# The value image of a deformable convolution, laid out by columns instead of rows

## The reference

```python
# layer 0: on xn = group_norm(x)
offsets = conv3x3(xn, offset_w); mod = 1 + tanh(conv3x3(xn, mod_w))
v = conv1x1(xn, kv_w)[:, C:]                    # the value image, 256 channels
sampled = bilinear(v, px = x + offset_x, py = y + offset_y) * mod   # 4 groups of 64 channels
x = x + conv1x1(sampled, out_w)
# layer 1: on xn = group_norm(x)
x = x + whiten(xn)     # mean and covariance in groups of 16 channels over the whole batch
```

## Time and profile before

| | |
|---|---|
| runs | 6293.51, 6298.68, 6304.76 us |
| median | 6298.68 us |
| span of the profiled execution | 7345.4 us, 66304 instructions |
| time recorded beside that span for the profiled execution | none but the span itself |
| mean granted TensorE clock | 0.796 |
| DRAM traffic | 1612.78 MB |

### The profile page before, as it was taken

The page is one execution under the profiler, slowest core; times in us unless marked ns, Lnnn a source line. Parts: engine busy times, 40 slices in busy tenths (PEclk is TensorE's granted clock), DMA queues, the critical chain, the costliest instruction groups (busy, mean ns, idle before and its releaser), DMA issues.

```text
span 7345.4 us, 66304 instructions
## 1 busy us (share of the span) xinstructions
PE 4556.6 (62%) x16380; PEld 2756.0 (38%) x16380; DVE 4512.5 (61%) x10805; ACT 979.6 (13%) x2075; POOL 4008.4 (55%) x4115
## 2 busy tenths in 40 slices
PE   5665666666666666665666666665667634337876
PEld 3333433343433343333334434343444422224322
DVE  7665666666766666666666656665666644446654
ACT  1111111111111111111111111111111101100000
POOL 0266666666666666565666666665666666660000
PEclk9877777887877878777888777777887766667999
DMA  8865666666666666666666656665666544445999
GB/s 279 277 195 195 222 216 194 221 220 212 220 205 212 216 203 223 206 210 203 199 216 222 211 195 217 211 205 183 195 198 200 186 139 134 127 130 229 421 421 415
DMA packets 931602, 1612.78 MB, mean 220 GB/s; under 512 B 80944, under 2 KB 605872, under 8 KB 929456
## 3 DMA queue, kind: packets, MB, share of 16 engines
q0 software_dynamic: 196608, 537.13, 22.5%
q10 hardware_dynamic: 595968, 536.90, 21.7%
q1 hardware_dynamic: 138928, 537.74, 21.5%
HBM read 1074.58 MB, written 536.87 MB: 219 GB/s over the span
## 4 chain that ended last, share of the span: by engine, by line
DVE 38%; another core or an unknown queue 27%; issue 16%; PE 7%; ACTq 6%; DMA 3%; DVEq 2%; ACT 1%; POOL 0%; SPq 0%; POOLq 0%
DVE patch L614 13%; DVE patch L619 7%; ACTq L1278 6%; DVE vring L497 3%; DVE bst L430 3%; DVE xr_mem L634 3%; DVE taps L509 2%; PE psO L1032 2%; PE psA L1000 2%; DVE samp_mem L625 1%; DVE weight L591 1%; DMA xs_mem<-x_dram 1%; DVE p_w L585 1%; ACT sampT L1179 1%
## 5 line engine op out<-in xcount | busy, mean ns | idle before, releaser
L899 POOL DMA_INDIRECT patch<-v,index_now x4096 | 4002.5, 977 | 2590.3 <-issue 1602.3
L1000 PE MATMUL psA<-wB,xa_mem 128*128 128x364 f32 x3824 | 1503.2, 536 | 768.4 <-issue 443.9
L614 DVE TENSOR_TENSOR patch<-patch,psI 128x512 f32<-128x512 f32 x2048 | 1264.9, 678 | 110.7 <-issue 55.2
L1000 PEld LDWEIGHTS psA<-wB,xa_mem 128*128 128x128 f32 x3824 | 780.7, 216 | 1363.7 <-issue 694.8
L1032 PE MATMUL psO<-sampT,wO_sb 128*128 128x512 f32 x2048 | 1171.5, 710 | 190.5 <-issue 181.4
L497 DVE TENSOR_TENSOR vring<-psA,biasB 128x256 f32<-128x256 f32 x956 | 397.7, 416 | 1375.2 <-remote 1198.7
L1046 PE MATMUL psT<-ident,xr_mem 128*128 128x128 f32 x2048 | 375.2, 334 | 886.3 <-DVE xr_mem L634 394.7
L1032 PEld LDWEIGHTS psO<-sampT,wO_sb 128*128 128x128 f32 x2048 | 456.1, 234 | 718.8 <-issue 709.2
L619 DVE TENSOR_TENSOR patch<-patch 128x512 f32<-128x512 f32 x1024 | 665.3, 691 | 94.7 <-remote 45.9
L1060 PE MATMUL psG<-x1T 128*128 128x129 f32 x4096 | 613.1, 306 | 154.2 <-issue 118.6
L634 DVE SCALAR_TENSOR_TENSOR xr_mem<-psO,bo_sb,xr_mem 128x512 f32<-128x512 f32 x512 | 361.1, 744 | 507.9 <-remote 411.2
(11 more groups left out here) (214 smaller groups left out, 2680.4 us busy)
## 6 DMA issues: line engine op xcount, KB each, us to landing
v<-vring ACTq DMA_DIRECT2D x128, 2048.0 KB
xa_mem<-x_dram SPq DMA_DIRECT2D x128, 1024.0 KB
xr_mem<-x_dram SPq DMA_DIRECT2D x128, 1024.0 KB
x<-xr_mem ACTq DMA_DIRECT2D x128, 1024.0 KB
xs_mem<-x_dram SPq DMA_DIRECT2D x112, 1024.0 KB
patch<-v,index_now POOLq DMA_INDIRECT x4096
patch<-x SPq DMA_DIRECT2D x64, 1024.0 KB, 13.1
out_dram<-patch ACTq DMA_DIRECT2D x64, 1024.0 KB, 32.6
```

The costliest lines, as they stand in the source:

```text
L614: times = eng.tensor_tensor(part, part, w4, ALU.mult)
L899: eng.indirect_dma_start(out=patch[n][:, t, :], out_offset=None, in_=v2_flat[k], in_offset=bass.IndirectOffsetOnAxis(ap=index_now[n][:, t: ...
L1000: mm = eng.matmul(conv_bank[wide][r][:, 0:NA], xa[m][j][:, c, r * W:(r + 1) * W], wB[:, c, :], start=(c == 0), stop=(c == CC - 1))
```

## The change

An entry of `v2` now holds a column and its right neighbour at one row, and the entries stand by columns: column, group, row. Two entries one after the other are rows y0 and y0+1 with both columns, again 1 KB for each sample. The gathers are the same in number and size; their address arithmetic has other factors, and the four weights stand in another order (corners 2 and 3 swapped). A column takes 256 KB (65536 numbers) and is followed by a gap of 2 KB (512 numbers), so neighbouring partitions write and read 264192 bytes apart, where it was 512 bytes.

The neighbour half of an entry is another partition's data. So ScalarE's copy within a partition is replaced by a product with the shift matrix on TensorE (`next_column`, 4 for each pair, 512 columns each) into a bank `psT`, and ScalarE copies it from there (`column_out`). `psT` was used by the two turns before; the new `_free` waits on TensorE order the three uses. The store of a pair is one run of 4 KB for each column and group, 512 runs of the same 2 MB. VectorE no longer waits for ScalarE's copy at the last row of a ring. Some set-up goes, two small DMAs fill the gaps once, and 16 semaphores of the output pass become one.

```diff
-VROW = G * W * ENT
-IMG = VROWS * VROW
+VCOL = G * H * ENT
+VPITCH = VCOL + 2 * PATCH
+IMG = W * VPITCH
...
-        vring = [sb(f"vring{m}", [P, QR + 1, G, 2, CG]) for m in range(2)]
+        vring = [sb(f"vring{m}", [P, G, QR, 2, CG]) for m in range(2)]
...
-                    if row == QR - 1:
-
-                        eng.wait_ge(v_dup, (b * PAIRS + i) * 5 + 2)
-                    dst = vring[m][:, row + 1, :, 0, :]
+                    dst = vring[m][:, :, row, 0, :]
...
-                    a[:, :, G:2 * G], float(VROW), ia, ALU.mult, ALU.add))
+                    a[:, :, G:2 * G], float(ENT), ia, ALU.mult, ALU.add))
...
+            def next_column(b, i, m, q, j, h):
+
+                eng.wait_ge(v_rows[j][h], b * PAIRS + i + 1)
+                eng.matmul(v_now[h], shift[:, 2, :], v_half(m, j, h, 0), start=True, stop=True)\
+                   .then_inc(shifted[j][h], 1)
...
-            def dup(b, i, m, j, rows):
-
-                low = j * ROWS + rows[0]
-                eng.wait_ge(v_row, (b * PAIRS + i) * QR + low + len(rows))
-                if low == 0:
-                    eng.activation(vring[m][:, 0, :, 0, :], vring[1 - m][:, QR, :, 0, :], ACT.Copy)\
-                       .then_inc(v_dup, 1)
-                eng.activation(vring[m][:, low:low + len(rows), :, 1, :],
-                               vring[m][:, low + 1:low + len(rows) + 1, :, 0, :], ACT.Copy)\
-                   .then_inc(v_dup, 1)
+            def column_out(b, i, m, j, h):
+
+                eng.wait_ge(shifted[j][h], b * PAIRS + i + 1)
+                eng.activation(v_half(m, j, h, 1), v_now[h], ACT.Copy).then_inc(v_next[j][h], 1)
...
-                eng.wait_ge(v_dup, (b * PAIRS + i) * 5 + 6)
-                eng.dma_start(v2_rows[k][:, bass.ds(row, 2 * NJ), :],
-                              vring[m][:, 0:QR, :, :, :].rearrange("p r g k e -> p (r g) (k e)"))\
+                eng.wait_ge(v_next[1][1], b * PAIRS + i + 1)
+                eng.dma_start(v2_cols[k][:, :, bass.ds(row, QR), :],
+                              vring[m][:, :, :, :, :].rearrange("p g r k e -> p g r (k e)"))\
```

More of the change, by code:

```diff
@@ L189, in deform_zca_kernel @@
         y_ld = [sem(f"y_ld{j}") for j in range(NY)]
[L190 removed]
+        y_mm = sem("y_mm")
         y_add = [sem(f"y_add{j}") for j in range(NY)]
@@ L272, in deform_zca_kernel, with v_half, before @@
         weight_now = psI[:, 512 - 2 * NJ * 4:512]
+        v_now = [bank[:, :].rearrange("p (g r e) -> p g r e", g=G, e=CG) for bank in psT]
+        def v_half(m, j, h, k):
+            low = j * ROWS + 2 * h
+            return vring[m][:, :, low:low + 2, k, :]
+        def before(b, i, m, q, j):
+            return (b, i, m, q, 0) if j == 1 else (b, i - 1, 1 - m, q - 1 + m, 1)
         block = ctx.enter_context(nc.Block())
@@ L328, in _ @@
                 eng.dma_start(dst, src).then_inc(const_ld, 16)
+            for gap in v2_gaps:
+                eng.dma_start(gap, x_v[0, :, 0, 0:VPITCH - VCOL]).then_inc(const_ld, 16)
             for n, store in enumerate((*v_st, *x1_st)):
@@ L1093, in pair @@
                             if three is not None:
+                                if turned:
+                                    next_column_free(*last_conv, 1)
+                                    if prepare and j == 1:
+                                        next_column_free(*last_conv, 0)
                                 turn_x1(*three)
@@ L1098, in pair @@
                                 conv((2,))
+                            if alongside and ca is not None:
+                                if three is not None:
+                                    x1_free(*three, 0)
+                                else:
+                                    next_column_free(*last_conv, 0)
+                                next_column(*here, 0)
                             if a is not None and j == 1:
@@ L1103, in pair @@
                             if one is not None:
+                                if three is None:
+                                    next_column_free(*last_conv, 1)
+                                if alongside and ca is not None:
+                                    next_column_free(*here, 0)
                                 turn_samples(*one)
@@ L1109, in pair @@
                                 conv(range(ROWS))
+                                samples_free(*one, 0)
+                                next_column(*here, 0)
+                            if ca is not None:
+                                if one is not None:
+                                    samples_free(*one, 1)
+                                else:
+                                    next_column_free(*last_conv, 1)
+                                next_column(*here, 1)
                 pairs(eng, pair)
@@ L1231, in pair @@
                                 x1_store(*three[:3])
-                        if prepare and j == 0:
+                        if g is None:
+                            if not (prepare and j == 1):
+                                pb, pi, pm_, pq_, pj = before(a, i + 1, 1 - m, q + m, j)
+                                column_out(pb, pi, pm_, pj, 1)
+                                if j == 0:
+                                    v_store(pb, k, pi, pm_)
+                            else:
+                                column_out(ca, ci, cm, 0, 1)
+                            if prepare and j == 0:
+                                root(ca)
+                            if a is not None and j == 1:
+                                modulation(a, i)
+                            column_out(ca, ci, cm, j, 0)
+                            if prepare and j == 1:
+                                column_out(ca, ci, cm, 1, 1)
+                                v_store(ca, 1 - k, ci, cm)
+                        elif ca is not None:
+                            if not (prepare and j == 0):
+                                column_out(ca, ci, cm, j, 0)
+                            if j == 1:
+                                modulation(a, i)
                             if one is not None:
                                 samples_out(*one)
[L1235 to L1238, removed]
+                            if prepare and j == 0:
+                                root(ca)
+                                column_out(ca, ci, cm, j, 0)
+                            column_out(ca, ci, cm, j, 1)
                             if j == 1:
                                 v_store(ca, 1 - k if last else k, ci, cm)
[L1241 to L1244, removed]
+                        else:
+                            if a is not None and j == 1:
+                                modulation(a, i)
+                            if one is not None:
+                                samples_out(*one)
                 pairs(eng, pair)
@@ L1256, in _ @@
             root(0)
[L1257 to L1260, removed]
+            for j, h in ((0, 0), (0, 1), (1, 0)):
+                column_out(0, 0, 0, j, h)
             image(None, None, 0, 1, 0)
```

81 lines of the change are left out of this document (52 added, 29 removed).

## The result

| | before | changed |
|---|---|---|
| median of the runs, us | 6298.7 (6293.5 to 6304.8) | 6322.4 (6321.7 to 6325.4) |
| ratio to before, 95% interval | | 1.0039 (1.0028 to 1.0050) |
| span of the profiled execution, us | 7345.4; again: 6282.3 | 6320.7 |

The change makes the kernel 24 us slower. It was forecast slower by 38 us.

A forecast was written before the change was run, and what follows sets the result against it. GpSimd's issue of gathers was taken to bound the unprofiled kernel. The first image's +38 us, all other terms 0, added to 6298.7 gave 6337 us, 0.6% slower, with 8 in 10 between 6170 and 6430 us.

The forecast's parts named there:

- The bound: Whole kernel, unprofiled: GpSimd's issue of gathers binds; start, gathers back to back and end make 6270.5 us against 6298.7.
- idle spells: Engines standing still with work ready in the first profile, such as 2.09 us on VectorE, read as instructions arriving late.
- First image: First value image, before any gather: four new products make TensorE the bound, 12.64 to 15.0 us a pair, +38 us.
- DMA bounds it: First value image before the change: DMA share 1.06 taken as the bound of its 12.64 us pairs, TensorE close behind.
- the likeliest case: First image pays, the rest is covered: 6337 us, reaching from 6325 to 6360, chance 0.44.
- Store, overlapped passes: Value store while gathers run: 1.0 us less DMA work a pair, gain 0; bounds nothing and 325 us.
- Products, overlapped passes: New TensorE products while gathers run: 5.7 us a pair, hidden, cost 0; +224 us if half a microsecond showed at each.
- ScalarE's index copy: Index copy for the second next block moves some 2 us later, covered by 20.4 us of gathers: 0.
- Gathers: Same number and bytes at a pitch of 264192 bytes, 0.403 us of DMA each: cost 0 unless DMA fills.
- The stall behind the stores: Engines delayed after each value store by its 4096 small runs; a rival held it real and going, 6175 us, chance 0.32.
- the faster case: Rival in which the delay after value stores goes: 1.45 us a pair over 112 pairs, 162 us, 6175 us, chance 0.32.
- The gather case: Rival: new pitch slows gathers, DMA binds from 0.70 us each, 6530 us at 0.75; chance 0.12 shared with exposed products.

The follow-up runs named there:

- e1: The kernel before, unedited, profiled once more: span 6282.3 us.
- e6: The kernel before with half as many gathers of 2 KB in place of 1 KB: 5088.5 us, ratio 0.8090 to the kernel before.
- e2: The changed kernel without the four shift products of a pair and their waits, layout kept: 6292.3 us, ratio 1.0000 to the kernel before.
- e8: The changed kernel without the shift products, and with half as many gathers, twice as large: 5087.5 us, ratio 0.8091 to the kernel before.
- e4: The changed kernel with its store of a pair again in 4096 runs of 512 bytes: 6314.9 us, ratio 1.0037 to the kernel before.
- e5: The changed kernel with each shift product done twice: 6367.1 us, ratio 1.0123 to the kernel before.
- e3: The changed kernel with no gap behind a column, partitions 262144 bytes apart: 6330.2 us, ratio 1.0064 to the kernel before.

## Why the prediction was right

**The bound.** "GpSimd's issue of gathers is the bound", read from 297.6 + 5231 + 741.9 = 6270.5 us against the median: right, though it stood on a disturbed profile. Shown by e1, where the gathers follow each other without a wait, and by e6, where fewer of them save 1200 us. The reading of the idle spells as late instructions was never tested; the idle spells were not there in any later profile, so they can't be explained from these runs.

**First image.** The mechanism was right and its size was off: the term was +38, between +31 and +58, and about 20 were measured, outside its own bounds. The step is "10.95 + 3.6 = 14.55 us a pair", for which 15.0 was taken. Measured are 13.89. The 10.95 us were TensorE's busy time in a window in which it still waited now and then, as in these rows of the second profile:

```profile
175.96 2.61 PE L1000 MATMUL psO<-wB,xa_mem 128*128 128x364 f32 x8
179.43 2.71 PE L1000 MATMUL psA<-wB,xa_mem 128*128 128x364 f32 x8 [0.86 <-DVE taps L509]
```

Without a stop the next group starts 2.45 us after this one, so 0.16 of its recorded 2.61 us lie under the next group. In front of a stop they count as busy time of their own, and the group behind the stop is recorded 0.10 us longer. That is some 0.26 us for each stop, an estimate from these rows, and two or three stops a pair fit the difference. Back to back, the old work is 9.80 + 0.64 = 10.44 us, and four products are 3.44, not 3.6, which included such an end. And no idle time came on top, where 0.45 us was allowed for it. So 1.24 us a pair and not 2.36: 20 us for 16 pairs, where 38 were forecast. The first gather starts 21.6 us later in the one pair of profiles, 18 us in the means; e2 and e8, without the products, have it at 296.5 and 295.5 us, level with the kernel before.

One reading of this stage did not hold. "DMA bounds it" was read from a share of 1.06: in e2 the share fell to 0.95 and the pair did not get shorter, and its chain goes through the single-buffered load and VectorE's work. The forecast did not suffer, since TensorE with the products takes longer than either. That the forecast of 6337 us was met to 15 us says little about this term, because the error of this term is small beside 6300 us: the measured median lies just under the 6325 us at which the likeliest case was to begin.

**Store, overlapped passes: 0.** Right, and tested three ways (e2, e4, e8). The store's DMA work fell more than the 1.0 us forecast: 0.374 x 125.03 / 9 = 5.20 us against 0.547 x 113.87 / 9 = 6.92. These are the queue rows of the nine pairs, changed kernel, then before:

```profile
q10 hardware_dynamic: 4752, 18.87, 37.4%
```

```profile
q10 hardware_dynamic: 37028, 18.88, 54.7%
```

So the Trainium skill's statement that 512 bytes are enough for line rate (DMA: Bandwidth & Descriptors, section Specifications) does not hold here: 2.10 MB in 6.92 us are 303 GB/s, a quarter below the 403 with runs of 4 KB, and e4 has 6.96 us for short runs at the changed kernel's own pace. It did not matter to the time, as DMA doesn't bind.

**Products, overlapped passes: 0.** Right: e5 doubles them for nothing there. TensorE's busy time grew from 3286.11 / (3603 / 32) = 29.2 to 31.9 us a pair, by 2.7 and not by the 5.7 that eight instructions of 716 ns gave. The waits that they bring do show on TensorE, and don't reach GpSimd (three rows of the changed kernel's timeline):

```profile
3524.51 2.48 DVE L625 TENSOR_TENSOR patch<-patch,psI 128x512 f32<-128x512 f32 x4 [5.14 <-DMA patch<-v,index_now]
...
3531.21 2.04 PE L1030 MATMUL psT<-vring,shift 128*128 128x512 f32 x2 [6.06 <-DVE vring L507]
...
3534.18 0.95 POOL L910 DMA_INDIRECT patch<-v,index_now  x1 [0.30 <-issue]
```

VectorE waits 5.14 us for a gather, so its rows come late, so the product waits 6.06 us, while GpSimd goes on at its 0.30 us.

**ScalarE's index copy: 0.** Right: 0.3 us of waiting in one place among 4096 gathers.

**Gathers: 0.** Right for the time. Their DMA work is 0.401 us each. Before it was 25.8% of 6282.3 / 4096 = 0.396 us, by the page of the second profile, and 0.403 by that of the first; the profiles with the new pitch lie between 0.400 and 0.406, so no cost of the pitch is shown:

```profile
q0 software_dynamic: 196608, 537.13, 25.8%
```

**The rivals.** The stall behind the stores was no property of the kernel, so there was nothing for the faster case to win. The gather case needed 0.30 us more DMA work for each gather and got 0.01 at most.

The later first gather accounts for 18 of the 24 us by the means, 21.6 by the one pair of profiles. In single profiles the mean gather is 981 ns before, 983 in e2, 984 in e4, 985 in the changed kernel, 987 in e3 and in e5, which is up to 25 us over 4096; runs of the kernel before alone spread over 15 us, so whether that is part of the change, and the rest of the 24 us, stays open.

None of the edits points to a version faster than both. What would pay is fewer gather instructions with the right data, and each of them, as this kernel uses it, takes one index for each partition.

## What to carry to other kernels

Add up each engine's time from one instruction's start to the next, with the gap, over the whole program, and set it beside the unprofiled median before believing in idle time: here that sum named GpSimd to within half a per cent, when its busy share was third. While one engine binds with room to spare on the others, as GpSimd did here, a change to DMA or TensorE work can cost or gain only in the stages where that engine doesn't run, so look for those first. A price read from busy time is safe only where the engine ran without stops. And before leaning on one profile that is longer than the runs, take a second.

## What was unexpected in the hardware

- An indirect DMA of 128 pieces costs GpSimd nearly the same for 1 KB and for 2 KB pieces: 946 ns in the median for both, 981 and 1030 ns in the mean (e1, e6); 2048 of them in place of 4096 took 1200 us off.
- Gathers with partitions 262144 bytes apart cost the DMA engines 0.404 us, 264192 bytes apart 0.400 to 0.406 in four profiles, 512 bytes apart 0.396 and 0.403 in two: no difference is shown.
- A store of 2.10 MB takes the DMA engines 6.92 and 6.96 us in runs of 512 bytes (e1, e4), 5.20 us in runs of 4 KB.
- In e2 and e8, the first image's pairs took 0.3 to 0.4 us longer than before (13.07 and 12.97 against 12.65) although the work of their stores was less.
